# Routed experts per sequence as 22 gathered blocks, and a first mixture block made without its row gather

## The reference, cut to what matters

```python
# level 0: 8 experts, hidden 1024, best 2 per token; level 1: 16 experts, hidden 512, best 3 per token
# level 3: 8 experts, hidden 512, best 2 per token, at most 320 tokens per expert
# level 2, the whole sequence is routed by its first token:
def _L2_ffn_ref(x, Wr, br, W1, b1, W2, b2):        # 8 experts, hidden 256
    scores0 = x[:, 0, :] @ Wr + br
    _, idx = jax.lax.top_k(scores0, 2)
    h = jnp.einsum('bsd,bkde->bkse', x, W1[idx]) + b1[idx][:, :, None, :]
    h = jax.nn.gelu(h, approximate=False)
    o = jnp.einsum('bkse,bkef->bksf', h, W2[idx]) + b2[idx][:, :, None, :]
    return jnp.sum(o, axis=1) / 2
```

## Time and profile before

| what | us |
|---|---|
| three runs | 1841.16 median, 1838.53 to 1845.12 |
| the profiled execution, its own time | 1834.88 |
| its span in the profile | 1833.0 |
| TensorE busy (share of the span) | 1553.4 (85%) |
| VectorE busy | 964.6 (53%) |
| ScalarE busy | 748.2 (41%) |
| GpSimd busy | 534.4 (29%) |

### The profile page before, as it was taken

The page is one execution under the profiler, slowest core; times in us unless marked ns, Lnnn a source line. Parts: engine busy times, 40 slices in busy tenths (PEclk is TensorE's granted clock), DMA queues, the critical chain, the costliest instruction groups (busy, mean ns, idle before and its releaser), DMA issues. The chain is left out here.

```text
span 1833.0 us, 44725 instructions
## 1 busy us (share of the span) xinstructions
PE 1553.4 (85%) x17451; PEld 1311.3 (72%) x17451; DVE 964.6 (53%) x2131; ACT 748.2 (41%) x1714; POOL 534.4 (29%) x699
## 2 busy tenths in 40 slices
PE   6999745799996999795999879997787998888894
PEld 5888644599975777674888768984675985666784
DVE  5666468611117888657222257664655773466323
ACT  3555455333433555351233236663133423445122
POOL 3444235032213443160444222220011210433341
PEclk9999877899998999897999989999887999898897
DMA  4211010198862111021899743330101119311696
GB/s 146 53 51 44 6 41 11 58 352 321 330 225 80 49 49 49 7 50 72 283 319 313 265 150 102 91 92 11 45 2 39 46 52 289 84 33 43 208 314 206
DMA packets 103107, 228.36 MB, mean 125 GB/s; under 512 B 36184, under 2 KB 56152, under 8 KB 95776
## 3 DMA queue, kind: packets, MB, share of 16 engines
q1 hardware_dynamic: 91008, 200.06, 33.8%
q0 software_dynamic: 8160, 22.29, 3.2%
q10 hardware_dynamic: 3776, 3.67, 0.6%
HBM read 206.12 MB, written 19.79 MB: 123 GB/s over the span
## 5 line engine op out<-in xcount | busy, mean ns | idle before, releaser
L2434 PEld LDWEIGHTS ps<-xt,w 128*128 128x128 f32 x1728 | 202.3, 192 | 37.8 <-issue 26.2
L2434 PE MATMUL ps<-xt,w 128*128 128x128 f32 x1728 | 211.2, 278 | 18.4 <-DMA w<-in_L_ffn_w 14.4
L2487 ACT ACTIVATE g<-ps,b 128x128 f32<-128x128 f32 x340 | 124.3, 367 | 245.1 <-PE ps L2434 220.5
L2444 PE MATMUL ps<-w,g 128*128 128x256 f32 x864 | 200.7, 379 | 0.3 <-ACT g L2487 0.3
L2444 PEld LDWEIGHTS ps<-w,g 128*128 128x128 f32 x864 | 157.5, 190 | 18.5 <-ACT g L2487 0.6
L2528 POOL DMA_INDIRECT results<-y,dest x85 | 83.8, 986 | 253.8 <-DVE y L2656 253.8
L2648 DVE COPY xt<-ps 128x256 f32<-128x256 f32 x85 | 36.1, 424 | 195.4 <-PE ps L2424 195.4
L2523 POOL DMA_INDIRECT x<-rows,token x85 | 82.7, 973 | 166.8 <-DVEq L2623 141.8
L2656 DVE COPY y<-ps 128x256 f32<-128x256 f32 x85 | 36.1, 425 | 161.9 <-PE ps L2444 161.9
L797 PE MATMUL ps<-c,w 128*128 128x258 f32 x512 | 93.4, 294 | 7.7 <-DVE pt L1108 6.4
L937 ACT ACTIVATE p<-sc,nmax 128x257 f32<-128x257 f32 x128 | 58.1, 503 | 81.3 <-DVE nmax L1065 81.3
(11 more groups left out here) (452 smaller groups left out, 3554.2 us busy)
## 6 DMA issues: line engine op xcount, KB each, us to landing
w<-in_L_ffn_w SPq DMA_DIRECT2D x124, 512.0 KB, 5.0
w<-in_L_ffn_w SPq DMA_DIRECT2D x46, 1024.0 KB, 5.1
c<-in_ctx SPq DMA_DIRECT2D x96, 258.0 KB, 2.7
rows<-in_w_L_xattn SPq DMA_DIRECT2D x32, 192.0 KB, 2.6
rows<-in_w_L_xattn SPq DMA_DIRECT2D x8, 768.0 KB
values<-v SPq DMA_DIRECT2D x8, 544.0 KB, 3.1
vx<-values SPq DMA_DIRECT2D x32, 136.0 KB, 3.4
c<-in_w_L_xattn SPq DMA_DIRECT2D x8, 514.0 KB
```

The costliest lines, as they stand in the source:

```text
L2434: mm = nc.tensor.matmul(hidden_bank(par, h), b.w1[:, par, c, h * P:(h + 1) * P], b.xt[:, par, c, :], start=c == 0, stop=c == DC - 1)
L2444: mm = nc.tensor.matmul(k.ps[:, YB + par, 0:D], b.g[:, par, h, :], b.w2[:, par, h, :], start=h == 0, stop=h == HC - 1)
L2487: nc.scalar.activation(b.g[:, par, h, :], hidden_bank(par, h), func, bias=b.b1[:, par, h:h + 1]).then_inc(s.g_ready, 1)
```

## The change

Level 2's experts no longer run through `gate` and `ffn` but through a new stage `by_sequence`. The eight experts' chosen sequences are sorted into 22 blocks of four sequences ((32·2 + 8·3)/4), each with one expert, and nothing of it passes through DRAM but the weights. Unused places of a block point to 32 spare columns in front of the tokens. Matmuls are plain fp32. The routing is the mixture's chain for two choices without the split of the places. The stage's core:

```diff
-                with buffers(k, raw1=[P, DC, hid], raw2=[P, hid // P, D]) as raw:
-                    early = [(raw.raw1[:], w1[0]), (raw.raw2[:], w2[0])]
-                    prepare(k, k.x, k.z, ht=k.ht, early=early, known=True, w_at=w.at, logits=w.gate)
-                    with buffers(k, comb=[P, NT, n_exp], comb_t=[n_exp, T]) as b:
-                        gate(k, w, n_exp, top, kind, b.comb, b.comb_t)
-                        ffn(k, w, n_exp, hid, w1, w2, func, b.comb, b.comb_t, k.x, b1=w.b1.rearrange("p e h -> p (e h)"), raw=raw)
+                with buffers(k, htx=[P, DC, S + T]) as b:
+                    prepare(k, k.x, k.z, ht=b.htx[:, :, S:], known=True, w_at=w.at, logits=w.gate)
+                    by_sequence(k, w, n_exp, hid, w1, w2, func, b.htx, k.x)
...
+        @block.sync
+        def _(sp):
+            sp.wait_ge(s.experts_ready, 1)
+            for n in range(NB):
+                e = sp.value_load(u.expert[0:1, n:n + 1], min_val=0, max_val=E - 1)
+                if n >= RING:
+                    sp.wait_ge(s.h_done, (n - RING + 1) * HC)
+                sp.dma_start(b.w1[:, n % RING], w1[ds(e, 1)].rearrange("a p c n -> (a p) c n")).then_inc(w1_loaded[n % RING], 16)
+                if n >= RING:
+                    sp.wait_ge(s.y_done, n - RING + 1)
+                sp.dma_start(b.w2[:, n % RING], w2[ds(e, 1)].rearrange("a p h d -> (a p) h d")).then_inc(w2_loaded[n % RING], 16)
...
+            def hidden(n):
+                pe.wait_ge(w1_loaded[n % RING], 16 * (n // RING + 1))
+                pe.wait_ge(s.x_ready, BT * (n + 1))
+                if n >= 2:
+                    pe.wait_ge(s.g_ready, HC * (n - 1))
+                for h in range(HC):
+                    for c in range(DC):
+                        mm = nc.tensor.matmul(hidden_bank(n, h), b.w1[:, n % RING, c, h * P:(h + 1) * P], b.x[:, n % 2, c, :],
+                                              start=c == 0, stop=c == DC - 1)
+                    mm.then_inc(s.h_done, 1)
+
+            def outputs(n):
+                pe.wait_ge(w2_loaded[n % RING], 16 * (n // RING + 1))
+                if n >= 2:
+                    pe.wait_ge(s.added, BT * (n - 1))
+                for c in range(DC):
+                    for h in range(HC):
+                        if c == 0:
+                            pe.wait_ge(s.g_ready, HC * n + h + 1)
+                        mm = nc.tensor.matmul(k.ps[:, YB + n % 2, c * P:(c + 1) * P], b.w2[:, n % RING, h, c * P:(c + 1) * P],
+                                              b.g[:, n % 2, h, :], start=h == 0, stop=h == HC - 1)
+                mm.then_inc(s.y_done, 1)
...
+            biases(0, s.first_bias)
+            hidden(0)
+            biases(1, s.second_bias)
+            hidden(1)
+            pe.wait_ge(s.sums_dve, 1)
+            for n in range(NB):
+                if 0 < n < NB - 1:
+                    hidden(n + 1)
+                outputs(n)
...
+            for n in range(NB):
+                seqs = positions(mybir.EngineType.Pool, n)
+                if n >= 2:
+                    pool.wait_ge(s.h_done, HC * (n - 1))
+                for j in range(BT):
+                    nc.gpsimd.tensor_copy(b.x[:, n % 2, :, j * S:(j + 1) * S], htx[:, :, ds(seqs[j], S)]).then_inc(s.x_ready, 1)
...
+            for n in range(NB):
+                seqs = positions(mybir.EngineType.DVE, n)
+                dve.wait_ge(s.y_done, n + 1)
+                y = k.ps[:, YB + n % 2, 0:D].rearrange("p (c t) -> p c t", c=DC)
+                for j in range(BT):
+                    if n or j:
+                        dve.wait_ge(s.added, n * BT + j)
+                    tile = b.sums[:, :, ds(seqs[j], S)]
+                    nc.vector.tensor_tensor(tile, tile, y[:, :, j * S:(j + 1) * S], ALU.add).then_inc(s.added, 1)
```

In the three mixtures block 0 is made by a product instead of a gather, and the experts' numbers move right behind the running sums:

```diff
             step(nc.vector.tensor_tensor_scan(f.end[:], k.ones[:, 0:E], f.count[:], 0.0, ALU.mult, ALU.add))
+            step(nc.vector.tensor_tensor(f.past[:], spread(f.end[:], NB, 1), spread(k.firsts[:, 0:NB], E, 2), ALU.is_le))
+            step(nc.vector.tensor_reduce(f.of[:], f.past[:], AX.X, ALU.add))
+            step(nc.vector.tensor_scalar(f.of[:], f.of[:], float(E - 1), None, ALU.min))
+            step(nc.vector.tensor_copy(u.expert[:], f.of[:]))
+            dve.sem_inc(s.experts_ready, 1)
...
+            step(nc.vector.tensor_reduce(f.low[:], f.at[:].rearrange("p n t -> p t n"), AX.X, ALU.min))
+            nc.vector.tensor_tensor(f.first[:], spread(k.row, NT, 1), spread(f.low[:], P, 2), ALU.is_equal).then_inc(s.first_ready, 1)
             step(nc.vector.tensor_copy(u.at[:], f.at[:]))
...
             for n in range(top):
                 nc.vector.tensor_tensor(r_.hot[:, n], spread(k.row, NT, 1), spread(f.lo[:, n], P, 2),
                                         ALU.is_equal).then_inc(s.hot_ready, 1)
-            step(nc.vector.tensor_tensor(f.past[:], spread(f.end[:], NB, 1), spread(k.firsts[:, 0:NB], E, 2), ALU.is_le))
...
-            dve.sem_inc(s.experts_ready, 1)
+            take_turned(0, 0)
             dve.wait_ge(s.rows_done, 1)
...
             keep_awake(k, spare, 6)
+            pe.wait_ge(s.first_ready, 1)
+            for c in range(DC):
+                for t in range(NT):
+                    mm = nc.tensor.matmul(k.ps[:, XB, c * P:(c + 1) * P], k.z[:, t, c * P:(c + 1) * P], f.first[:, t, :],
+                                          start=t == 0, stop=t == NT - 1)
+            mm.then_inc(s.xt_done, 1)
             for n in range(top):
                 pe.wait_ge(s.hot_ready, n + 1)
...
+            def first_body():
+                hidden(0, 0, 0, True)
+                pe.wait_ge(s.idx_ready, 1)
+                if b1 is not None:
+                    pe.wait_ge(s.comb_ready, 1)
+                    nc.tensor.transpose(k.ps[0:W, YB + 1, 0:P], f.comb[:].rearrange("p t e -> p (t e)"),
+                                        k.ident).then_inc(s.comb_turned, 1)
+                outputs(0, 0, 0, True)
+                turn(1, 1, 0)
...
-            keep_awake(k, spare, 8)
...
-            turn(0, 0, 0)
+            first_body()
             if b1 is not None:
                 pe.wait_ge(s.comb_spread, 1)
-            for slot in range(4):
-                body(slot, slot, 0, first=slot < 2)
+            body(1, 1, 0, first=True)
+            for slot in range(2, 4):
+                body(slot, slot, 0)
...
                 e = load_w1(par, par)
-                if par == 0:
-                    sp.wait_ge(x_loaded[0], 16)
+                if par == 1:
+                    sp.wait_ge(x_loaded[1], 16)
                 load_w2(e, par)
...
-            for n in range(4):
+            for n in range(1, 5):
                 gather(n)
             for n in range(NB):
-                if n + 4 < NB:
+                if n > 0 and n + 4 < NB:
```

More of the change, by code:

```diff
@@ L2324, in mixture @@
     down = k.down8 if E == 8 else k.down16
-    XB, HB, YB, IB = 0, 2, 6, 2
-    names = ("logits_done rounded step exp_done mask_ready ranks_done z_kept hot_ready rows_done idx_ready experts_ready "
+    XB, HB, YB, IB = 0, 2, 6, 7
+    names = ("logits_done rounded step exp_done mask_ready ranks_done z_kept first_ready hot_ready rows_done idx_ready experts_ready "
              "w1_loaded0 w1_loaded1 b1_loaded0 b1_loaded1 w2_loaded0 w2_loaded1 x_loaded0 x_loaded1 x_loaded2 x_loaded3 comb_ready comb_turned comb_spread bias_done "
@@ L2333, in mixture @@
                     at=[P, top, NT], lo=[P, top, NT], past=[P, NB, E], of=[P, NB],
-                    pads=[P, NB], comb=[P, NT, E], share=[P, top, NT], warm=[P, 1]) as f, \
+                    pads=[P, NB], comb=[P, NT, E], share=[P, top, NT], warm=[P, 1], low=[P, NT], first=[P, NT, P]) as f, \
             buffers(k, square=[P, D], mean=[P, NT], root=[P, NT], inverse=[P, NT]) as fin, \
@@ L2421, in turn @@
             def turn(n, slot, turns):
-                pe.wait_ge(x_loaded[slot], 16 * (turns + 1))
+                pe.wait_ge(x_loaded[slot], 16 * turns if slot == 0 else 16 * (turns + 1))
                 for c in range(DC):
@@ L2552, in over_experts, with take_turned @@
                 return spread(a[:], E, 2)
+            def take_turned(n, par):
+                dve.wait_ge(s.xt_done, n + 1)
+                nc.vector.tensor_copy(b.xt[:, par], k.ps[:, XB + par, 0:D].rearrange("p (c t) -> p c t", c=DC)).then_inc(s.xt_ready, 1)
             dve.wait_ge(*w.at)
@@ L2612, in _ @@
                                         ALU.is_equal).then_inc(s.hot_ready, 1)
-            step(nc.vector.tensor_tensor(f.past[:], spread(f.end[:], NB, 1), spread(k.firsts[:, 0:NB], E, 2), ALU.is_le))
-            step(nc.vector.tensor_reduce(f.of[:], f.past[:], AX.X, ALU.add))
-            step(nc.vector.tensor_scalar(f.of[:], f.of[:], float(E - 1), None, ALU.min))
-            step(nc.vector.tensor_copy(u.expert[:], f.of[:]))
-            dve.sem_inc(s.experts_ready, 1)
+            take_turned(0, 0)
             dve.wait_ge(s.rows_done, 1)
@@ L2662, in _ @@
```

(1 more changed line is left out.)

175 lines of the change are left out of this document (172 added, 3 removed).

## The result

| kernel | median us | runs | ratio to before, 95% |
|---|---|---|---|
| before | 1841.16 | 3 | |
| changed | 1790.92 (1787.73 to 1793.91) | 3 | 0.9718 [0.9688, 0.9748] |
| changed, second set | 1797.68 (before beside it 1844.2) | 6 | 0.9743 [0.9716, 0.9769] |

The account below looks back on a forecast made before the run. Level 2's experts were taken as TensorE-bound, mixtures by TensorE or with weight loads. Level 2 was to save 28.3 us (new loop 52.8, end 9.5), mixtures 0: from 1841.2 to 1812.9, forecast 1812, range 1797 to 1831.

Parts of the forecast that it names:

- VectorE's term of the loop's period: Level 2's loop: four register loads 1.1 us, additions 1.05, register operations 0.2, sum 2.35; period taken as 2.4.
- TensorE's own term: Level 2's loop: 8 hidden and 8 output records per block take TensorE 1.95 us.
- Rival A: Level 2's loop: TensorE-bound, register loads overlap; period 1.95, loop 43, gain 38, 1803 us; chance 0.22.
- start 2.2: Level 2's routing and loop start: offsets at 1408.2, first outputs at 1416 (1415 to 1418) on the time axis.
- loop 12.4: Level 2's loop: 22 periods of 2.4 us, 52.8 us in all.
- end 1.7: Level 2 after the last output: last additions 1.1, transposes 0.6, eight tiles 6.8, waits 1.0; 9.5 us.
- The mixtures, set to 0: Levels 0, 1 and 3, first block by product: gains and losses together 0, minus 5 to plus 5 us.
- The late load: Level 3: second w2 waits for block 1's gather, lands 5 us after issue, late for outputs(1); loss 2, gain 1.
- B: Level 2's loop: moderately register-bound, loads of 0.4 to 0.5 us; period 3.0, gain 15, 1826 us; chance 0.23.
- C: Level 2's loop: VectorE's loads cost as the longest SyncE row; period 4.2, loop 92.4, 1852 us; chance 0.05.
- D: Level 2's loop: TensorE's clock falls to half; 3.9 us per block, loop 86, 1845 us; chance 0.05.
- E: The mixtures lose: 5 us off A, the forecast or B; no side, and no chance, of its own.

Follow-up runs that it names:

- the first diff of the experiments: The changed kernel with VectorE's four column offsets in level 2's loop loaded by four one-register instructions instead of one of four: 1817.0 us, ratio 0.9847.

## Why the prediction was wrong

**The step that failed: VectorE's term of the loop's period, "four register loads ... four cost 1.1".** One instruction loads a block's four offsets in 0.344 us (the rows of L2754 above; the earlier trace rows held only loads of one register). VectorE's period is 1.64, not 2.35, and the bound passes to TensorE. I counted values where I should have counted instructions; `positions` makes one call for all four (the first diff of the experiments). Split in four, as I had thought, the loop has a period of 2.61, and the time is 1817, near my forecast of 1812. The other terms of VectorE's sum came out right only together: the four additions take 1.28, forecast 1.05, and the register operations, which I had added as 0.2, lie between them.

**TensorE's own term, 1.95, was too long too.** The earlier trace rows give the busy time of 16 records with the modelled end of the last. Back to back, 16 records take 1.79 from start to start. Rival A had the right bound and the wrong size. Of the loop's 12.4 us below, 9.9 are the first step (22 periods of 2.4 and not 1.95) and 2.5 this one.

The stretch of level 2, 111.4 us before, took 66.8 (1392.24 to 1459.03), not 83.1. The 16.3 us are: start 2.2 (outputs(0) begins 18.6 us after the stage's first operation, forecast 20.8, in the execution where the clock fell later and for less long; 22.8 in the second set), loop 12.4 (40.4 from there to the last additions, forecast 52.8; 22 x 1.79 is 39.4, the other 1.0 lie in blocks with a longer period, three of which waited for weights, 0.8 in all), end 1.7 (7.8, forecast 9.5).

**The mixtures, set to 0 (minus 5 to plus 5):** 4.7 us less by the runs, about 2 by the mean of the traces. Level 0: the first product took 5.3, forecast 7.0 out of 3.75 to 7.4; hidden(1) comes 25.0 us after the second operation on the logits, 28.0 before: 3.0 earlier, forecast 0.7. Level 1: hidden(0) comes 6.0 us earlier, hidden(1) 3.1, and some 1.5 of it are left at the end; what takes the rest was not tried. Level 3: a loss of 2.5 by the means, forecast as a loss of up to 2. The late load is felt at outputs(1), as I had said, by 0.77 us, but more at hidden(2), by 2.00 us, which I had not priced; before, block 1 waited 1.16.

**The base.** I took the profiled execution of before to be 6.3 us below its median. That of the changed kernel lies 3.0 above its own. So 9.3 of the 50.2 us are in no trace; the second set gives 46.5.

**The rivals.** B (period 3.0) and C (4.2) fall by the 0.344; the longest row was 0.596. D falls: the clock in the loop is 0.99. But the clock did act in the loop's start, by 4.4 us from one execution to another. I had allowed it 3 us there (1415 to 1418 for the first outputs); the slower start, 22.8 us, would be 1418.0, the end of that, and the faster lies 1.2 us below its beginning. E falls in sign for the sum and holds for level 3. Against A I had argued that little can hide a load behind dependent additions. That was right: 0.20 us of it, beside the last addition, whatever the number of loads. There was only a quarter as many.

## What to carry to other kernels

Before you price a helper's loads, count the instructions it emits, and find the period of each engine apart; here the two nearest differed by 0.15 us, so the answer turned on one instruction. For back-to-back groups take the spacing of their starts, not their busy time. A wait placed to let one transfer pass holds back every later one of its queue: price it at the consumers of all of them (here 0.77 us at the first and 2.00 at the next), not at the first alone.

## What the hardware showed that I had not expected

- Register loads out of SBUF on VectorE: 0.309 us for one register, 0.528 for two, 0.344 for four by one instruction (0.320 for four on GpSimd). The cost follows neither the registers nor the instructions; why two cost more than four stays open. The Trainium skill (Runtime: NRT & Kernel Launch, Instruction fetch mechanics) gives about 200 ns per register even in bulk, in a passage on loads from HBM. By an estimate with that figure four would be 0.8; for these loads out of SBUF the measurement decides, 0.344.
- A load starts beside the last of the additions ahead of it (0.025 us after its start, in three kernels), so only that addition's 0.20 us overlap; the profile shows the rest as idle time of VectorE.
- The granted clock took two courses over the same instructions at level 2's start (0.79 and 1.00 in the same us), 4.4 us apart at the loop. Level 0's first product, too, ran once at 1.00 and eight times slower behind the same idle time. Why one and not the other stays open.
- It also fell, to 0.63 on average, in a stretch that begins with bias products of 8 partitions, with TensorE busy throughout. Whether the few partitions or something before them is the cause was not tried.
